# Deformable convolution: patches cut from a turned image in DRAM instead of strips turned tile by tile

## The chip, the cores and the metric

One NeuronCore of a Trainium2 chip runs the whole program. The metric is device time in microseconds (us), as a median of repeated runs. All data is float32.

## The reference

The input `x` is 4 images of 128 channels and 32x32 pixels. Two residual layers follow each other.

1. `x = x + mix(gn(x))`: `gn` normalises groups of 4 channels. `mix` forms the cosine similarity of all 1024 pixels with each other, takes relu and square, and multiplies the result with a 1x1 convolution of the normalised image.
2. `x = x + relu(deform(h))` with `h = gn(x)`: a 3x3 convolution `w1` and a 3x3 convolution `w2` give 72 offset planes (4 groups of channels, 9 taps, y and x). For each pixel, tap and group `h` is read bilinearly at the shifted place (zero outside the image), and a 3x3 convolution `wd` sums the 9 taps.

```
val = gather(y0, x0) * (wy0 * wx0) + gather(y0, x0 + 1) * (wy0 * wx1)
    + gather(y0 + 1, x0) * (wy1 * wx0) + gather(y0 + 1, x0 + 1) * (wy1 * wx1)
out = relu(einsum('ogck,bgckhw->bohw', wd, val))
```

## The kernel before

**Sampling as matrix products.** No gather is used. A tile is 4 rows of the image (128 pixels), so a batch has 8 tiles (`ROWT`). A tile has 8 blocks of 4x4 pixels. With offsets of at most 2 pixels, all that a block reads lies in an 8x8 patch (64 cells) around it, taken from an image whose rows run on into each other and which is wrapped at its ends. For each pixel, tap and group VectorE (DVE) forms the 64 bilinear weights (`tents`, `weights`, lines 1439 to 1474, into `wpix`, in 5 groups of taps). TensorE (PE) turns them from pixel to cell rows (`turn_weights`, line 719) into `psT`, and ScalarE (ACT) copies each group to `wcell` (`evacuate`, line 1005). PE then multiplies the patches with them (`sample`, line 742) in two halves per tile into `psV`, ACT copies these into `val` (line 1018), and `dconv` or, in the last batch, `dconv_tile` applies `wd`.

**How the patches arise before the change.** `wrap_image` on GpSimd (POOL) copies the normalised image `hpad` into `hring` (line 468). For each tile `cut_strips` copies two strips of it, even and odd blocks (line 482). `cut_windows` on PE turns these with 4 transposes into a `psT` bank (line 709). ACT copies the bank into `hwin` (line 999). The even blocks then lie in partitions 0 to 63 and the odd ones in 64 to 127. As `sample` wants each block in both halves, `cross` sends each half to the other with two transfers of 128 KB on the SP queue (line 365). `hwin` has two buffers, for even and odd tiles.

**Order.** All engines follow an order written out by hand. A batch is 72 slots, 9 per tile (`SLOTS`). The text calls the turns of one tile T0, T1, W, T2, T3, T4 (weights 0 to 4, W for the windows), in slots 0, 1, 2, 3, 5, 6 of the tile (`TURN_SLOT`), and S0, S1 the two halves of `sample` for the tile before, in slots 2 and 6. The six turns use the two `psT` banks in turn; each waits until ACT has emptied the bank two turns back (`turns`, line 694).

Between these slots stands the work of later batches: scores and mixing of batch b+2 (`SCORE`, `MIX`, slots 0 to 26; ACT relu, POOL square at line 459), normalising batch b+1 for its second layer (slots 23 to 28), its two convolutions in split precision (`conv_front`: DVE forms row combinations at lines 1263 and 1267 with an ACT copy at line 975 between, PE multiplies at line 540, slots 36 to 41 and 49 to 54), and the offsets: POOL wraps them, the SP queue shifts them by tap with 9 transfers of 8 rows (`shift_offsets`, line 316), PE turns them (line 661, slots 65 and 67). Ahead of batch 0 stands a lead of 72 slots that does the same for batches 0 to 2. Batch 3 has no later batch beside it; there PE has sampling and `dconv_tile` alone.

The SP queue is one ordered list: `shift_offsets(0)`, then for each batch `cross` of tiles 0 to 6, `shift_offsets(b + 1)`, `cross` of tile 7, and the stores.

`sim` (two buffers of 128x1024) holds the squared scores and later, as `off_ring`, the offsets.

Of the kernel before, what the change touches and what calls it, by code (L numbers as in the profile page):

```python
# [37 lines left out]
def mix_deform_kernel(nc, x, W0, b0, w1, b1, w2, b2, wd, out):  # L38
# [17 lines left out]
    HRING = NPIX + 2 * RING  # L56
    V, PAIRS = 4, H // 2
# [5 lines left out]
    TURNS = ["taps 0", "taps 1", "windows 0", "taps 2", "taps 3", "taps 4"]  # L63
    TURN_SLOT = {0: "taps 0", 1: "taps 1", 2: "windows 0", 3: "taps 2", 5: "taps 3", 6: "taps 4"}
# [9 lines left out]
    with ctx:  # L74
# [68 lines left out]
        hring = sb("hring", [P, HRING])  # L143
# [5 lines left out]
        strips = sb("strips", [P, NBLK // 2, 2, CELLS])  # L149
# [79 lines left out]
        def middle_rows(b):  # L229
# [12 lines left out]
            "stat2_done cells_ready w2_ordered off_wrapped off_shifted off_saved hring_done strips_done val_wrapped "  # L242
            "g_off g_offT g_pos g_stat g_h g_hT g_hTs g_place g_shift g_d1 g_f1 g_tent g_zero g_cur g_plane g_turn g_planeT "
            "g_sample g_acc g_conv g_relu g_out g_stored "
            "swap_ready own_ready crossed_even crossed_odd dist_done fold_done tent_done weights_done turned turn_free "
            "sampled val_free dconv_done orelu_done yout_done settled grid_ready out_first out_second").split()}
        out_sems = [s["out_first"], s["out_second"]]
        off_scr = nc.dram_tensor("off_scr", [B, NOFF, NPIX], F32, kind="Internal").ap()

# [16 lines left out]
        LEAD_IMAGE = 37  # L266
# [71 lines left out]
        def _(sp):  # L338
# [21 lines left out]
            def cross(b, t):  # L360

                sp.wait_ge(s["own_ready"], ROWT * b + t + 1)
                for r in range(2):
                    here, there = (slice(CELLS * h, CELLS * (h + 1)) for h in (r, 1 - r))
                    sp.dma_start(hwin[there, t % 2, :, 1, :], hwin[here, t % 2, :, 0, :])\
                        .then_inc(s["crossed_odd" if t % 2 else "crossed_even"], 16)
# [12 lines left out]

            shift_offsets(0)  # L380
            for b in range(B):
                for t in range(ROWT - 1):
                    cross(b, t)
                if b + 1 < B:
                    shift_offsets(b + 1)
                else:
                    store_tile(0)
                cross(b, ROWT - 1)
# [21 lines left out]
        def _(pool):  # L410
# [52 lines left out]
            def wrap_image(b):  # L463

                pool.wait_ge(s["h_done"], b + 1)
                if b > 0:
                    pool.wait_ge(s["strips_done"], 2 * ROWT * b)
                pool.tensor_copy(hring[:, RING:RING + NPIX].rearrange("p (r c) -> p r c", c=WID),
                                 hpad[:, 1:1 + H, 1:1 + WID]).then_inc(s["hring_done"], 1)
                pool.wait_ge(s["hring_done"], 3 * b + 1)  # L470
                pool.tensor_copy(hring[:, 0:RING], hring[:, NPIX:NPIX + RING]).then_inc(s["hring_done"], 1)
                pool.tensor_copy(hring[:, RING + NPIX:HRING], hring[:, RING:2 * RING]).then_inc(s["hring_done"], 1)
                pool.wait_ge(s["hring_done"], 3 * b + 3)

            def cut_strips(b, t):

                if b > 0 or t > 0:
                    pool.wait_ge(s["turned"], (ROWT * b + t - 1) * TGROUPS + TURNS.index("windows 0") + 1 + TURNED0)
                for odd in range(2):
                    at = P * t + BLK * odd  # L480
                    src = hring[:, at:at + SUP * WID].rearrange("p (r m c) -> p m r c", r=SUP, c=SUP)
                    pool.tensor_copy(strips[:, :, odd, :].rearrange("p m (r c) -> p m r c", c=SUP), src)\  # L482
                        .then_inc(s["strips_done"], 1)
# [16 lines left out]
            def batch_steps(b):  # L500
                nxt = b + 1 if b + 1 < B else None
                for t in range(ROWT + 1):
                    for k in range(K):
# [5 lines left out]
                        if t < ROWT - 1 and k == 5:  # L509
                            cut_strips(b, t + 1)  # L510
                        if nxt is not None and t == ROWT - 1 and k == 1:
                            wrap_image(nxt)
                        if nxt is not None and t == ROWT - 1 and k == 5:
                            cut_strips(nxt, 0)
# [6 lines left out]
            for n in range(SLOTS):  # L521
                if n in SCORE:
                    square(0, SCORE.index(n))
                if n == LEAD_IMAGE:
                    wrap_image(0)
                    cut_strips(0, 0)
# [9 lines left out]
        def _(pe):  # L536
# [100 lines left out]
            def conv(b, which, w_p, width, step):  # L637

                for m in (2 * step, 2 * step + 1):
# [63 lines left out]
            def cut_windows(b, t, part):  # L703

                pe.wait_ge(s["strips_done"], 2 * (ROWT * b + t) + 2)
                bank = turns(b, t, f"windows {part}")
                for v in range(4):
                    strip = strips[:, v, :, :].rearrange("p e q -> p (e q)")
                    last = pe.transpose(bank[:, v * C:(v + 1) * C], strip, ident[:, :])  # L709
                last.then_inc(s["turned"], 1)  # L710
# [12 lines left out]
            def sample(b, t, v):  # L723

                n = VGROUPS * t + v
                if v == 0:

                    pe.wait_ge(s["turn_free"], freed(ROWT * b + t, TGROUPS - 1))
                    pe.wait_ge(s["crossed_odd" if t % 2 else "crossed_even"], 32 * (ROWT // 2 * b + t // 2 + 1))
# [107 lines left out]
            def batch_steps(b):  # L837
# [5 lines left out]
                for t in range(ROWT):  # L843
                    for k in range(K):
                        n = K * t + k
                        if k in TURN_SLOT:
                            kind, i = TURN_SLOT[k].split()
                            (turn_weights if kind == "taps" else cut_windows)(b, t, int(i))
# [11 lines left out]
                        if prep is not None:  # L860
                            for what in PREP.get(n, ()):
                                prepare(prep, what)
                        if nxt is not None:
# [37 lines left out]
            for n in range(SLOTS):  # L901
                mix_front(0, n)
                for b, table in ((1, PREP_SECOND), (2, PREP_THIRD)):
                    for what in table.get(n, ()):
                        prepare(b, what)
                conv_front(0, n, LEAD, None)
# [11 lines left out]
        def _(act):  # L918
# [65 lines left out]
            def evacuate(b, t, what):  # L984

                idx = TURNS.index(what)
                kind, i = what.split()
                i = int(i)
# [9 lines left out]
                if kind == "windows":  # L998
                    act.activation(hwin[:, t % 2, :, 0, :], bank.rearrange("q (m c) -> q m c", c=C), ACT.Copy)\
                        .then_inc(s["turn_free"], 1)  # L1000
                    act.wait_ge(s["turn_free"], freed(ROWT * b + t, idx))
                    act.nop().then_inc(s["own_ready"], 1)
                else:
                    taps = TAPS[i]
                    act.activation(wcell[:, t % 2, taps[0]:taps[-1] + 1, :, :].rearrange("q k h p -> q (k h p)"),  # L1005
                                   bank[:, 0:len(taps) * G // 2 * P], ACT.Copy).then_inc(s["turn_free"], 1)
# [48 lines left out]
            def batch_steps(b):  # L1055
                nxt = b + 1 if b + 1 < B else None
                for t in range(ROWT):
                    for k in range(K):
# [10 lines left out]
                        if nxt is not None:  # L1069
                            conv_front(nxt, n, STEADY)  # L1070
                        if b == LAST and t >= 4 and k == 4:
# [24 lines left out]
            for n in range(SLOTS):  # L1096
                mix_front(0, n)
                for b, table in ((1, PREP_SECOND), (2, PREP_THIRD)):
                    for what in table.get(n, ()):
                        prepare(b, what)  # L1100
                conv_front(0, n, LEAD)
# [15 lines left out]
        def _(dve):  # L1117
# [62 lines left out]
            def normalise_x1(b):  # L1180
# [5 lines left out]
                else:  # L1186
                    dve.wait_ge(s["hring_done"], 3 * b)
# [507 lines left out]
```

## Time and profile before

| | us |
|---|---|
| median of 3 runs | 474.54 |
| lowest, highest run | 472.19, 474.91 |
| profiled execution, its own time | 476.88 |
| span of its trace, first to last instruction | 475.2 |

The profiled execution lies 2.34 us above the median. Its mean granted TensorE clock is 0.962 of full speed. Every row of the trace comes from this one execution; times in rows count from the start of the span. In the rows an engine's busy time is the union of its instructions, and the idle time before a group is put down to what ended it.

### The profile page before, as it was taken

To read this page: it belongs to the slowest core of one execution; us is meant where nothing else is said; L and a number is where in the kernel's file an instruction comes from. 1 tells how busy PE (TensorE), PEld (TensorE's weight loads), DVE (VectorE), ACT (ScalarE), POOL (GpSimd) and SP (SyncE) were. 2 spreads that over 40 slices of the span, in tenths; PEclk is the share of its full clock that TensorE was granted. 3 is DMA by queue.
4 is the path that set the end of the run, shared out by engine and by line. 5 is a ranking of instruction groups with operands and counts; after the bars stand their busy time and mean duration, and the time that the engine had idled before them with its cause. 6 is when DMAs were issued, how large, how long until landed. Compare 5 with 4: busy or idle time off the path is not lost.

```text
span 475.2 us, 9943 instructions
## 1 busy us (share of the span) xinstructions
PE 423.5 (89%) x3983; PEld 306.1 (64%) x3983; DVE 344.4 (72%) x586; ACT 230.5 (49%) x416; POOL 131.3 (28%) x171
## 2 busy tenths in 40 slices
PE   7897999989997889899999789799789898979996
PEld 6654657656664665778666566677556566757876
DVE  4994776949999987398755988096977927599701
ACT  3442245155564554443666554433754643167762
POOL 5562472003883111102774110201301120022200
PEclk9997999999999899999999899889988997999999
DMA  7100000021111011311111111401211122022221
GB/s 254 63 0 0 0 3 0 1 50 23 23 23 24 14 20 25 62 25 44 23 22 23 24 24 23 96 12 51 51 23 24 24 41 56 33 57 47 46 63 31
DMA packets 22763, 17.25 MB, mean 36 GB/s; under 512 B 2044, under 2 KB 21244, under 8 KB 22716
## 3 DMA queue, kind: packets, MB, share of 16 engines
q1 hardware_dynamic: 22652, 16.46, 14.9%
q8 instruction: 33, 0.54, 0.4%
q10 hardware_dynamic: 64, 0.13, 0.2%
q14 instruction: 14, 0.11, 0.1%
HBM read 3.74 MB, written 3.28 MB: 15 GB/s over the span
## 4 chain that ended last, share of the span: by engine, by line
PE 54%; DVE 29%; ACT 5%; issue 5%; SPq 3%; POOL 1%; DMA 1%; ACTq 1%; DVEq 0%; POOLq 0%
PE psB L768 10%; PE psB L540 9%; PE psT L719 7%; DVE wpix L1474 6%; PE psV L742 6%; PE psA L540 5%; PE psA L631 4%; DVE combo L1263 3%; DVE tent L1455 2%; PE psT L709 2%; SPq L316 2%; DVE tent L1449 2%; ACT wcell L1005 2%; PE psB L793 2%; DVE combo_p L1267 2%
## 5 line engine op out<-in xcount | busy, mean ns | idle before, releaser
L1005 ACT ACTIVATE wcell<-psT 128x512 f32<-128x512 f32 (+1 forms) x160 | 83.9, 552 | 72.1 <-PE psT L719 70.6
L1474 DVE TENSOR_TENSOR wpix<-tent 128x512 f32<-128x512 f32 (+1 forms) x160 | 104.1, 701 | 14.2 <-PE psT L719 13.1
L719 PE MATMUL psT<-ident,wpix 128*128 128x128 f32 x576 | 88.4, 285 | 13.1 <-ACT wcell L1005 12.0
L719 PEld LDWEIGHTS psT<-ident,wpix 128*128 128x128 f32 x576 | 68.2, 147 | 36.8 <-issue 29.0
L482 POOL COPY strips<-hring 128x256 f32<-128x256 f32 x64 | 40.8, 664 | 145.3 <-PE psT L709 145.2
L459 POOL TENSOR_TENSOR sim<-rel 128x512 f32<-128x512 f32 x48 | 61.8, 1309 | 66.4 <-ACT rel L955 66.4
L1018 ACT ACTIVATE val<-psV 128x576 f32<-128x576 f32 x64 | 44.0, 688 | 22.1 <-PE psV L742 19.7
L768 PE MATMUL psB<-val,wd_sb 128*128 128x256 f32 x216 | 51.6, 394 | 0.0
L742 PE MATMUL psV<-wcell,hwin 64*32 64x144 f32 x2048 | 47.6, 296 | 0.9 <-ACT val L1018 0.9
L631 PE MATMUL psA<-sim,scratch 128*128 128x512 f32 x96 | 47.5, 619 | 0.7 <-POOL sim L459 0.6
L768 PEld LDWEIGHTS psB<-val,wd_sb 128*128 128x128 f32 x216 | 41.0, 195 | 8.6 <-issue 3.1
L540 PE MATMUL psA<-combo_p,w_p 128*128 128x512 f32 (+1 forms) x144 | 43.4, 443 | 1.1 <-DVE combo_p L1267 1.1
L540 PE MATMUL psB<-g_p 128*128 128x512 f32 x144 | 41.6, 424 | 0.0
L955 ACT ACTIVATE rel<-psB 128x512 f32<-128x512 f32 x48 | 28.5, 598 | 24.1 <-PE psB L540 20.2
L540 PE MATMUL psB<-combo_p,w_p 128*128 128x512 f32 (+1 forms) x144 | 38.1, 411 | 0.0
L742 PEld LDWEIGHTS psV<-wcell,hwin 64*32 64x32 f32 x2048 | 28.0, 108 | 13.8 <-issue 10.9
L975 ACT ACTIVATE combo_p<-combo 128x544 fp32r<-128x544 f32 x32 | 20.8, 657 | 28.5 <-DVE combo L1263 28.5
L540 PEld LDWEIGHTS psA<-combo_p,w_p 128*128 128x128 f32 (+1 forms) x144 | 24.9, 183 | 12.0 <-issue 2.6
L709 PE MATMUL psT<-ident,strips 128*128 128x128 f32 x128 | 20.4, 283 | 12.7 <-ACT wcell L1005 12.7
L540 PEld LDWEIGHTS psB<-g_p 128*128 128x128 f32 x144 | 26.0, 191 | 8.2 <-issue 3.4
L1267 DVE TENSOR_TENSOR combo_p<-combo,combo_p 128x544 fp32r<-128x544 f32 x32 | 25.3, 792 | 6.2 <-ACT combo_p L975 5.4
L540 PEld LDWEIGHTS psB<-combo_p,w_p 128*128 128x128 f32 (+1 forms) x144 | 23.3, 166 | 9.9 <-DVE combo_p L1267 0.2
(196 smaller groups left out, 521.9 us busy)
## 6 DMA issues: line engine op xcount, KB each, us to landing
hwin<-hwin SPq DMA_DIRECT2D x64, 128.0 KB, 2.4
x_all<-x SPq DMA_DIRECT2D x1, 1536.0 KB, 10.9
out<-yout SPq DMA_DIRECT2D x12, 128.0 KB, 1.8
off_scr<-sim SPq DMA_DIRECT2D x4, 288.0 KB
combo<-sim SPq DMA_DIRECT2D x32, 32.0 KB
val<-w SPq DMA_DIRECT2D x1, 576.0 KB, 6.2
wd_sb<-wd SPq DMA_DIRECT2D x1, 576.0 KB
x_all<-x SPq DMA_DIRECT2D x1, 512.0 KB, 3.3
```

The costliest lines, as they stand in the source:

```text
L459: pool.tensor_tensor(own.sim[:, i % 2, j * HALF:(j + 1) * HALF], own.rel[:, j, :], own.rel[:, j, :], ALU.mult)\
L482: pool.tensor_copy(strips[:, :, odd, :].rearrange("p m (r c) -> p m r c", c=SUP), src)\
L540: last = pe.matmul(dst, left[l], right[r], start=start and i == 0, stop=stop and i == 2)
L631: last = pe.matmul(own.sums[:, j, :], own.gx[:, i, :], own.sim[:, i % 2, j * HALF:(j + 1) * HALF], start=i == 0, stop=i == QT - 1)
L709: last = pe.transpose(bank[:, v * C:(v + 1) * C], strip, ident[:, :])
L719: last = pe.transpose(bank[:, at:at + P], wpix[:, t % 2, k, 2 * h:2 * h + 2, :].rearrange("p g q -> p (g q)"), ident[:, :])
L742: last = pe.matmul(bank[g * CG:(g + 1) * CG, e, :, m, :], hwin[rows, t % 2, u // 2, (u + r) % 2, g * CG:(g + 1) * CG], w[:, :, :, BLK * u: ...
L768: last = pe.matmul(bank, wd_sb[:, k * C:(k + 1) * C], val[:, k, at:at + 2 * P], start=k == 0, stop=k == K - 1)
L1005: act.activation(wcell[:, t % 2, taps[0]:taps[-1] + 1, :, :].rearrange("q k h p -> q (k h p)"), bank[:, 0:len(taps) * G // 2 * P], ACT.Cop ...
L1018: act.activation(dst, src, ACT.Copy).then_inc(s["val_free"], 1)
L1267: dve.tensor_tensor(combo_p[:, 1, v], combo[:, v % 2], combo_p[:, 0, v].bitcast(F32), ALU.subtract)\
L1474: dve.tensor_tensor(w, ty, tx, ALU.mult).then_inc(s["weights_done"], 1)
```

## The change

The turns of the strips go from the tiles to once per batch. POOL copies `hpad` flat (`copy_flat`, slot 34 of the lead, 28 of a batch). PE turns the image of a batch with 8 transposes into both banks of `psB` (`turn_image`, slot 38 or 33). ACT copies the two banks into buffer 0 of `sim` (`copy_image`, slot 39 or 34). The SP queue stores it as 1024 rows of 512 bytes, with wrapped ends, in DRAM (`store_image`), lays that out as 8 strips of 36 rows of 8 pixels in a second DRAM tensor (`lay_image`, two transfers DRAM to DRAM), and for each tile brings the patches with four transfers of 128 KB (`windows`). These wait until the tile two before has been sampled. W, `cut_strips`, the ring and `cross` are gone, so a tile has 5 turns. New waits: the third row product of the first convolution waits for the copied image (it reuses `psB`), and the offsets wait until the image is stored (they reuse `sim`).

```diff
-    TURN_SLOT = {0: "taps 0", 1: "taps 1", 2: "windows 0", 3: "taps 2", 5: "taps 3", 6: "taps 4"}
+    TURN_SLOT = {0: "taps 0", 1: "taps 1", 3: "taps 2", 5: "taps 3", 6: "taps 4"}
...
-        LEAD_IMAGE = 37
+        LEAD_IMAGE, STEADY_IMAGE, IMAGE_TILE = 38, 33, 5
+        LEAD_FLAT, STEADY_FLAT = 34, 28
...
+            def store_image(b):
+                sp.wait_ge(s["image_copied"], 2 * (b + 1))
+                ring = h_ring[b]
+                sp.dma_start(ring[RING:RING + NPIX, :].rearrange("(i q) c -> q i c", q=P), h_px).then_inc(s["image_stored"], 16)
+                sp.dma_start(ring[0:RING, :], h_px[P - RING:P, QT - 1, :]).then_inc(s["image_stored"], 16)
+                sp.dma_start(ring[RING + NPIX:HRING + BLK, :], h_px[0:RING + BLK, 0, :]).then_inc(s["image_stored"], 16)
+            def lay_image(b):
+                sp.wait_ge(s["image_stored"], 3 * 16 * (b + 1))
+                for odd in range(2):
+                    sp.dma_start(h_scr[b].rearrange("(m e) q c -> e m (q c)", e=2)[odd].rearrange("m (r n) -> m r n", n=SUP * C),
+                                 h_ring[b][BLK * odd:BLK * odd + IMAGE_ROWS * WID, :]
+                                 .rearrange("(r m c) n -> m r (c n)", m=NBLK // 2, c=SUP)).then_inc(s["image_laid"], 16)
+            def windows(b, t):
+                n = ROWT * b + t
+                if t == 0:
+                    sp.wait_ge(s["image_laid"], 2 * 16 * (b + 1))
+                if n >= 2:
+                    sp.wait_ge(s["sampled"], VGROUPS * (n - 1) + SAMPLED0)
+                for odd in range(2):
+                    src = h_scr[b][:, BLK * SUP * t:BLK * SUP * t + CELLS, :].rearrange("(m e) q c -> e q m c", e=2)[odd]
+                    for r in range(2):
+                        dst = hwin[CELLS * r:CELLS * (r + 1), t % 2, :, (odd + r) % 2, :]
+                        sp.dma_start(dst, src).then_inc(s["windows_odd" if t % 2 else "windows_even"], 16)
...
+            store_image(0)
+            lay_image(0)
+            for t in range(2):
+                windows(0, t)
             shift_offsets(0)
             for b in range(B):
+                for t in range(2, ROWT):
+                    if t == IMAGE_TILE and b + 1 < B:
+                        store_image(b + 1)
+                    if t == IMAGE_TILE + 1 and b + 1 < B:
+                        lay_image(b + 1)
+                    if t == ROWT - 1 and b + 1 < B:
+                        shift_offsets(b + 1)
+                    if t == ROWT - 1 and b == LAST:
+                        store_tile(0)
+                    windows(b, t)
...
+                    for t in range(2):
+                        windows(b + 1, t)
                     for m in range(4):
                         store(b, m)
...
+            def copy_flat(b):
+                pool.wait_ge(s["h_done"], b + 1)
+                if b > 0:
+                    pool.wait_ge(s["image_turned"], 2 * b)
+                pool.tensor_copy(h_flat[:, :].rearrange("p (r c) -> p r c", c=WID), hpad[:, 1:1 + H, 1:1 + WID])\
+                    .then_inc(s["flat_done"], 1)
...
+                    if kx == 0 and which == 0 and v == 2:
+                        pe.wait_ge(s["image_copied"], 2 * (b + 1))
...
+            def turn_image(b):
+                pe.wait_ge(s["flat_done"], b + 1)
...
+                for i in range(QT):
+                    last = pe.transpose(psB[:, i // 4, i % 4 * C:(i % 4 + 1) * C], h_flat[:, i * P:(i + 1) * P], ident[:, :])
+                    if i % 4 == 3:
+                        last.then_inc(s["image_turned"], 1)
...
+            def copy_image(b):
...
+                for j in range(2):
+                    act.wait_ge(s["image_turned"], 2 * b + j + 1)
+                    act.activation(h_px[:, 4 * j:4 * j + 4, :].rearrange("p i c -> p (i c)"), psB[:, j, :], ACT.Copy).then_inc(s["image_copied"], 1)
...
+                if which:
+                    dve.wait_ge(s["image_stored"], 3 * 16 * (b + 1))
```

## Rows read from the trace of the kernel before

**Rows 1.** The page: busy us, share of the span, instructions.
```profile
PE 423.5 (89%) x3983; PEld 306.1 (64%) x3983; DVE 344.4 (72%) x586; ACT 230.5 (49%) x416; POOL 131.3 (28%) x171
```

**Rows 2.** The page: the chain that ended last, by engine and by line.
```profile
PE 54%; DVE 29%; ACT 5%; issue 5%; SPq 3%; POOL 1%; DMA 1%; ACTq 1%; DVEq 0%; POOLq 0%
PE psB L768 10%; PE psB L540 9%; PE psT L719 7%; DVE wpix L1474 6%; PE psV L742 6%; PE psA L540 5%; PE psA L631 4%; DVE combo L1263 3%; DVE tent L1455 2%; PE psT L709 2%; SPq L316 2%; DVE tent L1449 2%; ACT wcell L1005 2%; PE psB L793 2%; DVE combo_p L1267 2%
```

**Rows 3.** Groups by line: busy us, mean ns; idle us before, releaser.
```profile
L709 PE MATMUL psT<-ident,strips 128*128 128x128 f32 x128 | 20.4, 283 | 12.7 <-ACT wcell L1005 12.7
```

**Rows 4.** PE in order of time, batch 3, one tile: start, us, instructions.
```profile
421.05 1.06 PE L719 MATMUL psT<-ident,wpix 128*128 128x128 f32 x8 [0.28 <-DVE wpix L1474]
422.52 0.63 PE L709 MATMUL psT<-ident,strips 128*128 128x128 f32 x4 [0.40 <-ACT wcell L1005]
423.07 0.72 PE L742 MATMUL psV<-wcell,hwin 64*32 64x144 f32 x32
...
425.60 0.72 PE L742 MATMUL psV<-wcell,hwin 64*32 64x144 f32 x32
426.25 0.98 PE L719 MATMUL psT<-ident,wpix 128*128 128x128 f32 x7
```

**Rows 5.** PE in order of time, batch 3, a tile with dconv.
```profile
439.06 0.60 PE L709 MATMUL psT<-ident,strips 128*128 128x128 f32 x4
439.59 0.72 PE L742 MATMUL psV<-wcell,hwin 64*32 64x144 f32 x32
```

**Rows 6.** PE in order of time, batch 1, a tile with scores.
```profile
224.09 0.60 PE L709 MATMUL psT<-ident,strips 128*128 128x128 f32 x4
224.53 0.60 PE L719 MATMUL psT<-ident,wpix 128*128 128x128 f32 x4
```

**Rows 7.** PE in order of time, first convolution in batch 0.
```profile
162.02 0.63 PE L709 MATMUL psT<-ident,strips 128*128 128x128 f32 x4 [0.59 <-ACT wcell L1005]
...
163.23 1.73 PE L540 MATMUL psA<-combo_p,w_p 128*128 128x512 f32 x6
```

**Rows 8.** ACT in order of time, the same stretch.
```profile
160.17 0.66 ACT L975 ACTIVATE combo_p<-combo 128x544 fp32r<-128x544 f32 x1 [3.02 <-DVE combo L1263]
...
161.30 1.07 ACT L1005 ACTIVATE wcell<-psT 128x512 f32<-128x512 f32 x2
```

**Rows 9.** PE in order of time, second convolution in batch 0.
```profile
173.65 0.63 PE L709 MATMUL psT<-ident,strips 128*128 128x128 f32 x4 [1.51 <-ACT wcell L1005]
...
178.90 0.41 PE L719 MATMUL psT<-ident,wpix 128*128 128x128 f32 x2
```

**Rows 10.** ACT in order of time, the same stretch.
```profile
178.17 1.56 ACT L1005 ACTIVATE wcell<-psT 128x512 f32<-128x512 f32 x3
```

**Rows 11.** DVE `tent` in batch 2: ns min/median/max, first and last start.
```profile
L1455 DVE SCALAR_TENSOR_TENSOR tent<-tent x3: 758/832/833, 329.2 to 339.6; 128x576 f32<-128x576 f32 x3
```

**Rows 12.** The lead, PE and POOL in order of time.
```profile
67.84 2.43 PE L540 MATMUL psA<-combo_p,w_p 128*128 128x512 f32 x9 [0.65 <-DVE combo_p L1267]
...
67.47 2.61 POOL L459 TENSOR_TENSOR wpix<-wcell 128x512 f32<-128x512 f32 x2 [0.35 <-ACT wcell L955]
70.02 1.53 POOL L468 COPY hring<-hpad 128x1024 f32<-128x1024 f32 x1
```

**Rows 13.** The lead, ACT and the SP queue in order of time.
```profile
72.16 0.66 ACT L975 ACTIVATE combo_p<-combo 128x544 fp32r<-128x544 f32 x1 [2.29 <-DVE combo L1263]
...
94.89 3.41 SPq L316 DMA_DIRECT2D combo<-sim  x5
```

**Rows 14.** DMA: 40 slices of the span; issues; packets between 94 and 103 us.
```profile
DMA  7100000021111011311111111401211122022221
GB/s 254 63 0 0 0 3 0 1 50 23 23 23 24 14 20 25 62 25 44 23 22 23 24 24 23 96 12 51 51 23 24 24 41 56 33 57 47 46 63 31
...
hwin<-hwin SPq DMA_DIRECT2D x64, 128.0 KB, 2.4
...
DMA packets 228, 0.59 MB, mean 66 GB/s; under 512 B 84, under 2 KB 84, under 8 KB 228
```

More of the change, by code:

```diff
@@ L461, in square @@
                         .then_inc(s["sim_done"], 1)
-            def wrap_image(b):
+            def copy_flat(b):
                 pool.wait_ge(s["h_done"], b + 1)
                 if b > 0:
[L467 to L483, printed above, removed]
+                    pool.wait_ge(s["image_turned"], 2 * b)
+                pool.tensor_copy(h_flat[:, :].rearrange("p (r c) -> p r c", c=WID), hpad[:, 1:1 + H, 1:1 + WID])\
+                    .then_inc(s["flat_done"], 1)
             def wrap_offsets(b):
@@ L508, in batch_steps @@
                             wrap_offsets(nxt)
[L509 to L514, printed above, removed]
+                        if nxt is not None and n == STEADY_FLAT:
+                            copy_flat(nxt)
                         if t in (1, ROWT) and k == 8:
@@ L701, in turns @@
                 return psT[:, (TGROUPS * t + idx) % 2, :]
[L703 to L710, printed above, removed]
+            def turn_image(b):
+                pe.wait_ge(s["flat_done"], b + 1)
+                if b > 0:
+                    pe.wait_ge(s["orelu_done"], 4 * (b - 1) + ORELU0)
+                if b + 1 < B:
+                    pe.wait_ge(s["rel_done"], 2 * QT * (b + 2 if b else 1))
+                for i in range(QT):
+                    last = pe.transpose(psB[:, i // 4, i % 4 * C:(i % 4 + 1) * C], h_flat[:, i * P:(i + 1) * P], ident[:, :])
+                    if i % 4 == 3:
+                        last.then_inc(s["image_turned"], 1)
             def turn_weights(b, t, i):
@@ L862, in batch_steps @@
                                 prepare(prep, what)
+                        if nxt is not None and n == STEADY_IMAGE:
+                            turn_image(nxt)
                         if nxt is not None:
@@ L905, in _ @@
                         prepare(b, what)
+                if n == LEAD_IMAGE:
+                    turn_image(0)
                 conv_front(0, n, LEAD, None)
@@ L986, in evacuate @@
                 idx = TURNS.index(what)
-                kind, i = what.split()
-                i = int(i)
+                i = int(what.split()[1])
                 if idx == 0:
@@ L997, in evacuate @@
                 bank = psT[:, (TGROUPS * t + idx) % 2, :]
[L998 to L1006, printed above, removed]
+                taps = TAPS[i]
+                act.activation(wcell[:, t % 2, taps[0]:taps[-1] + 1, :, :].rearrange("q k h p -> q (k h p)"),
+                               bank[:, 0:len(taps) * G // 2 * P], ACT.Copy).then_inc(s["turn_free"], 1)
+            def copy_image(b):
+                if b > 0:
+                    act.wait_ge(s["off_saved"], 16 * b)
+                    act.wait_ge(s["off_shifted"], SHIFTS * b)
+                if b + 1 < B:
+                    act.wait_ge(s["mix_done"], QT * (b + 2 if b else 1))
+                for j in range(2):
+                    act.wait_ge(s["image_turned"], 2 * b + j + 1)
+                    act.activation(h_px[:, 4 * j:4 * j + 4, :].rearrange("p i c -> p (i c)"), psB[:, j, :], ACT.Copy)                        .then_inc(s["image_copied"], 1)
             def take_samples(b, t, v):
@@ L1070, in batch_steps @@
                             conv_front(nxt, n, STEADY)
+                        if nxt is not None and n == STEADY_IMAGE + 1:
+                            copy_image(nxt)
                         if b == LAST and t >= 4 and k == 4:
@@ L1100, in _ @@
                         prepare(b, what)
+                if n == LEAD_IMAGE + 1:
+                    copy_image(0)
                 conv_front(0, n, LEAD)
```

40 lines of the change are left out of this document (15 added, 25 removed).

## The prediction

> **What bounds the kernel now.** I read the page first. TensorE is busy for 89% of the span and no other engine is over 72% [rows 1]. That is a mean over stages, so I took the chain of waits next: 54% of it lies on PE and 29% on DVE [rows 2], so time taken from PE comes back where PE ends last, and is lost where DVE or ACT does. The turning of the windows, W, holds 2% of the chain by itself. The list of groups gives its whole size: 20.4 us of PE time in 128 transposes, and 12.7 us in which PE stood idle before them until ACT had emptied a bank of `psT` [rows 3]. Last I went through PE and ACT in order of time, stage by stage, to see which wait ends last there.
>
> **What W is worth, stage by stage.** In the new order S0 follows T1 directly, and T2 and T3 wait for banks that were filled one turn earlier than before, so no wait for a bank gets longer.
>
> - Batch 3, tiles without `dconv` (four, the last one half): T0 and T1 end at 422.11, PE idles 0.40, and W takes 0.55 until S0 starts at 423.07 [rows 4]. Both go, as S0 needs nothing of T0's bank; T0 is copied while S0 runs. I take 0.9 of the 0.95, so 3.6. The period of 5.20 [rows 4] becomes 4.3.
> - Batch 3, tiles with `dconv_tile` (four): PE never idles, and W takes 0.53 from its start to S0's [rows 5]. 4 x 0.53 = 2.1.
> - Batch 1, slots 0 to 26: PE is full with scores and mixing. W takes 0.44 [rows 6]; three tiles, 1.3.
> - Batch 0, same slots: DVE is on the chain, not PE. What comes is relief from POOL's copying of strips. Where POOL runs no squares, `tent` line 1455 takes 0.758 us alone and 0.833 beside such copies [rows 11]; two DVE operations per tile touch them, 0.15 per tile. Three tiles, 0.5. The first three tiles of batch 2 are bound by DVE too: 0.5. Nothing and three times as much are the ends.
> - First convolution (batches 0, 1 and 2): PE idles 0.59 for a bank and W takes 0.56, with the next row product only at 163.23 [rows 7]. ACT is late, as it waited until 160.17 for DVE's last row combination [rows 8]. S0 then waits only for the copy of the samples before, which ACT makes ahead of that bank. The new `copy_image` puts two copies, 1.07 as in [rows 8], between them; T2, one row product later, covers it. 1.1 each, 3.3; and 0.7 in batch 2, where W of tile 3 also holds up the ACT copy from which the first row product comes.
> - Second convolution (three times): PE idles 1.51 before W at 173.65 [rows 9], which looks like the best gain, but is not: T4 at 178.90 starts just after ACT's copy of T2 ends (178.17 + 0.58) [rows 9, 10], and ACT copies in order behind DVE's row combinations. What PE wins at 173.65 it loses at 178.90. I take 0.25 each, 0.7.
> - Tile 7 of batch 0: W and its wait, of which the offsets' turns give half back, 0.45. In batches 1 and 2 PE waits there for the shifted offsets; nothing.
>
> Sum: 3.6 + 2.1 + 1.3 + 0.5 + 0.5 + 3.3 + 0.7 + 0.7 + 0.45 = 13.15 saved. POOL's strips, ACT's copies of W and the crossings leave engines that bind nowhere; they are costed at nothing beyond the relief above.
>
> **What comes in.** (a) `turn_image`, 8 transposes, 1.06 as the first line of [rows 4]. In batches 0 to 2 it stands before the first convolution, where PE waits for row combinations anyway; these are made after `hpad`, as is the flat copy. That cover is a tie, 0 to 0.3 each; I take 0. (b) In the lead the cover is too short. The flat copy comes before the square that ran from 67.47, and lasts 1.53 [rows 12], so to 69.0 at most; turning ends at 69.9, and the convolution that began at 67.84 [rows 12] starts 1.5 to 2 late. (c) `copy_image(0)` stands behind the last of ACT's four copies of row combinations, which ends at 72.82 [rows 13]: image copied at 73.9. The third row product, before at 73.00 and now about 1.6 later, just meets that.
>
> (d) The path through DRAM in the lead. The SP queue must store the image, lay it, and issue eight window transfers before `shift_offsets(0)`, which began at 94.89 [rows 13]. An issue takes 3.41/5 = 0.68; a 128 KB transfer lands 2.4 after its issue [rows 14]. The store has four times the data: about 4.6 with its three issues, so 78.5. Laying moves 8 x 36 x 4 KB = 1.18 MB. In the first slice all 16 DMA engines, busy for 7 tenths, moved 254 GB/s [rows 14], so 363 GB/s busy throughout: 3.3 us on 16 engines. But not every transfer uses 16. Between 94 and 103 us nine shifts of 8 rows and one store of 72 rows moved 144 large pieces and closed with 84 small packets [rows 14]: 9 x 8 and 12. So a transfer runs on as many engines as divide its rows. The laying's outermost extent is 4 strips, with 36 pieces in each; whether the pieces spread, no row tells. With 4 engines laying takes 13.0, with 16 it takes 3.3. I take 13.0, as in all these the closing packets divide the outer extent. With 2 us to land, the image lies at 93.5, the windows are issued by 98.9, and the shift starts 4.0 late. Of that PE waited 0.6 less, so the lead loses 3.4, which includes (b). Ends: 1.6 (16 engines) and 9 (DRAM to DRAM at two thirds of that rate).
>
> The Trainium skill's page "DMA: Bandwidth & Descriptors", section "Why a DMA increments its semaphore by 16 and not by 1", speaks against the change here: it lets a transfer use the largest number up to 16 that divides the slowest extent of both sides, which for 4 strips gives 4. By that rule the sum stays as it is; by the other reading it would be 1.8 better.
>
> (e) In later batches the same laying starts when the window transfers of tile 5 are issued, 20 us ahead of its use, and is over before the next shift. Nothing. (f) Window transfers: four issues and a landing are 3 x 0.68 + 2.4 = 4.4 from the trigger; one after another they would take 9.6. The trigger is the end of S1 of tile t-2; S0 of tile t comes two periods after the S0 that stands 3.25 before this end [rows 4]. At a period of 4.3 that leaves 2 x 4.3 - 3.25 = 5.35, in tiles with scores over 15. I take 4.4, since the two crossings, issued 0.6 apart, both land in 2.4: transfers overlap. So nothing waits. (g) Stores of batch b now queue behind the windows of the next batch, which wait for S1 of tile 7; output rows have two buffers and `dconv` lasts longer than the delay. Nothing.
>
> Net: -13.15 + 3.4 = -9.75. The profiled execution, 476.88 in all, would become 467.1. It lies 2.34 above the median of 474.54, so against the runs I forecast **464.8 us**.
>
> **Rivals.** *More comes back (454).* W's 2% of the chain (9.5 us) and all 12.7 us of idle time before it [rows 2, 3] are saved and the laying runs on 16 engines: -22.2 + 1.6 = -20.6. For it: waits often vanish together. Against: rows 9 and 10. Chance 0.13.
>
> *The time is handed to DVE and ACT (472).* In the three batches with convolutions each gain is met by a later wait, as in [rows 9, 10], and only batch 3 keeps its 5.7: -5.7 + 3.4 = -2.3. For it: DVE's 29% of the chain. Against: rows 6 and 7, where PE has work queued and nobody late. Chance 0.13.
>
> *The windows come late (slower, 486).* Place: the first product of S0. If four transfers take L, the period cannot be below (L + 3.25)/2. In batch 3 and the first tiles of batch 2 ten tiles have periods of 5.2 (six) or 6.1 (four). Without batch 3's share the rest nets -7.45 + 3.4, about -4. The loss 6 x (P - 5.2) + 4 x (P - 6.1) eats this at P = 6.0, so L = 8.7; that is the point. At L = 11 P is 7.1, the loss 15.6, the time 486. For it: one after another gives 9.6. Against: they overlap today. Chance 0.08.
>
> **Numbers.** The forecast has 0.66; its own range is 459 to 470 (saving 10.5 to 16, lead 1.6 to 9, not both ends at once). To leave out no more than 2 in 10 I reach to 456 and 471, into the first two rivals. About 1%, 4.7 us, is what a measurement tells from no change, so faster means under 469.8: 0.62 of the forecast, 0.13 and a little of the second, 0.78. Same: 0.13. Slower: the third and a lead that loses more than 16, 0.09.
>
> **What would show it.** Right: tiles of batch 3 at periods near 4.3 and 5.6; in the second convolution T4 still starting on ACT's copy; `shift_offsets(0)` about 4 us later, with the laying's packets over 13 us. Wrong: PE idle before S0 with a DMA as releaser; the laying done in 4 us; PE waiting for POOL's flat copy in batches 0 to 2; a lower granted clock where PE now idles more.

## The result, and the profile after

The changed kernel takes **459.79 us** (median of 4 runs, 459.05 to 463.93) beside 474.73 for the kernel before, measured beside it: a ratio of 0.969, 95% interval 0.965 to 0.974. Five later runs (E0 below) gave 461.14 and 0.970 (0.968 to 0.972). The forecast was 464.8, the range 456 to 471. The direction and the main mechanism held; 4 to 5 us more came back than the sum had, and some terms of the sum missed in opposite directions.

The profiled execution took 459.05 us, span 457.0, mean granted clock 0.970. From its page: busy time, the chain by engine and by line [rows 1, 2], and from the groups by line the one that holds the window transfers' only wait.

```profile
PE 405.2 (89%) x3887; PEld 291.9 (64%) x3887; DVE 339.5 (74%) x586; ACT 215.6 (47%) x392; POOL 90.0 (20%) x99
...
PE 46%; DVE 32%; DMA 6%; SPq 5%; issue 4%; ACT 4%; POOL 1%; DVEq 0%; ACTq 0%; POOLq 0%
...
L762 PE MATMUL psV<-wcell,hwin 64*32 64x144 f32 x2048 | 47.2, 294 | 3.9 <-ACT val L1045 3.5 <-DMA hwin<-h_scr 0.4
```

PE's share of the chain fell from 54% to 46%; DVE, DMA and the SP queue took it over. PE waited for windows 0.4 us in all in this execution, so step (f) and the third rival are settled.

PE in batch 3: a tile without `dconv` [rows 4], then one with it [rows 5].

```profile
411.11 1.09 PE L739 MATMUL psT<-ident,wpix 128*128 128x128 f32 x8
412.13 0.72 PE L762 MATMUL psV<-wcell,hwin 64*32 64x144 f32 x32
...
414.26 0.41 PE L739 MATMUL psT<-ident,wpix 128*128 128x128 f32 x2 [0.39 <-ACT wcell L1021]
...
415.25 1.09 PE L739 MATMUL psT<-ident,wpix 128*128 128x128 f32 x8
...
425.15 0.38 PE L739 MATMUL psT<-ident,wpix 128*128 128x128 f32 x2
425.46 0.72 PE L762 MATMUL psV<-wcell,hwin 64*32 64x144 f32 x32
...
430.82 0.38 PE L739 MATMUL psT<-ident,wpix 128*128 128x128 f32 x2
```

S0 follows T1 with no wait. The period is 415.25 - 411.11 = 4.14, against a forecast of 4.3; with `dconv` it is 430.82 - 425.15 = 5.67, against 5.57.

First convolution of batch 1, made during batch 0: PE [rows 7] and ACT [rows 8].

```profile
158.09 1.71 PE L555 MATMUL psA<-combo_p,w_p 128*128 128x512 f32 x6
160.50 0.72 PE L762 MATMUL psV<-wcell,hwin 64*32 64x144 f32 x32 [0.69 <-ACT val L1045]
161.15 1.25 PE L555 MATMUL psA<-combo_p,w_p 128*128 128x512 f32 x4
...
159.12 0.66 ACT L998 ACTIVATE combo_p<-combo 128x544 fp32r<-128x544 f32 x1 [3.02 <-DVE combo L1294]
159.68 0.67 ACT L1045 ACTIVATE val<-psV 128x576 f32<-128x576 f32 x1
160.24 1.07 ACT L1033 ACTIVATE sim<-psB 128x512 f32<-128x512 f32 x2
```

As forecast, S0 waits only for the copy of the samples before, and the image's two copies (1.07) stand behind that. Ahead of this stretch lies a cost that the sum had at nothing. DVE's first two row combinations after `hpad`, before and then changed, with POOL's flat copy:

```profile
153.26 1.36 DVE L1263 TENSOR_TENSOR combo<-hpad 128x544 f32<-128x544 f32 x2
```

```profile
151.54 2.20 DVE L1294 TENSOR_TENSOR combo<-hpad 128x544 f32<-128x544 f32 x2
151.57 1.59 POOL L502 COPY h_flat<-hpad 128x1024 f32<-128x1024 f32 x1 [8.86 <-DVE hpad L1219]
```

Both start from `hpad`. The second combination takes 1.56 beside the flat copy, 0.72 without it (in the lead, where POOL's squares run beside it, 1.56 in both kernels). T0 of tile 4, which waits for ACT behind these combinations, comes 4.37 after `hpad` in place of 3.53, in batches 0 and 1 of every trace of the changed kernel and of its variants.

Second convolution of the same batch, PE and ACT [rows 9, 10]:

```profile
176.42 0.41 PE L739 MATMUL psT<-ident,wpix 128*128 128x128 f32 x2 [0.88 <-ACT wcell L1021]
...
175.70 1.55 ACT L1021 ACTIVATE wcell<-psT 128x512 f32<-128x512 f32 x3
```

T4 still starts just after ACT's first copy (175.70 + 0.58). The lead [rows 12, 13]: PE, then ACT, then the SP queue; last, 10 us of the laying by windows (span, busy of PE, PEld, DVE, ACT and POOL, granted clock, DMA share, GB/s).

```profile
66.17 1.09 PE L728 MATMUL psB<-ident,h_flat 128*128 128x128 f32 x8 [1.46 <-POOL h_flat L502]
67.01 1.72 PE L555 MATMUL psA<-combo_p,w_p 128*128 128x512 f32 x6
...
100.73 0.34 PE L678 MATMUL psA<-ident,combo 72*128 72x72 f32 x2 [1.06 <-DMA combo<-sim]
...
70.25 1.07 ACT L1033 ACTIVATE sim<-psB 128x512 f32<-128x512 f32 x2
...
75.32 1.26 SPq L376 DMA_DIRECT2D h_scr<-h_ring  x2
89.69 5.44 SPq L391 DMA_DIRECT2D hwin<-h_scr  x8
95.18 3.49 SPq L320 DMA_DIRECT2D combo<-sim  x5
...
78.00:88.00 10.00, 10.00 (x61) 7.59 (x60) 7.16 (x12) 5.44 (x9) 0.00 (x0) 1.00 0.26 104
```

The work ahead of the change already ran 2.48 us earlier in this execution than in that of before (`hpad` at 60.68 against 63.16; the work up to there is the same), so stages are compared by their own lengths. From PE's first weight turn of one batch to that of the next (the lead from `hpad`, batch 3 to the end of the span), with the second profiled run of the changed kernel (E0 below), and with two kernels that come later (E12 and E10):

```
          before   changed          forecast   measured       E12      E10     E10-E12
lead       45.78    47.74  46.68     +3.4     +1.95 +0.90     45.79    47.40    +1.61
batch 0   111.18   108.19 109.75     -2.3     -2.99 -1.43    112.68   108.16    -4.52
batch 1   107.37   102.28 102.33     -2.65    -5.09 -5.04    106.77   101.37    -5.40
batch 2    89.28    84.69  84.64     -2.55    -4.59 -4.64     85.49    79.98    -5.51
batch 3    58.39    53.44  53.70     -5.7     -4.95 -4.69     58.71    52.70    -6.01
```

Two sizes were off: the lead lost less, and batches 1 and 2 gained nearly twice as much as forecast.

### The profile page after: what moved, and what is told of

The parts are those of the page before. It is cut to its first block, busy times and chain, and to the rows that moved or that the text cites. A ratio compares the mean times of both kernels' runs of the same rounds, so it can differ in the third digit from the quotient of the medians.

```text
span 457.0 us, 9689 instructions
## 1 busy us (share of the span) xinstructions
PE 405.2 (89%) x3887; PEld 291.9 (64%) x3887; DVE 339.5 (74%) x586; ACT 215.6 (47%) x392; POOL 90.0 (20%) x99
## 4 chain that ended last, share of the span: by engine, by line
PE 46%; DVE 32%; DMA 6%; SPq 5%; issue 4%; ACT 4%; POOL 1%; DVEq 0%; ACTq 0%; POOLq 0%
PE psB L788 10%; PE psB L555 9%; PE psT L739 7%; DVE wpix L1507 7%; PE psV L762 5%; DVE combo L1294 4%; PE psA L646 4%; DMA h_scr<-h_ring 3%; SPq L320 3%; DVE combo_p L1298 2%; DVE tent L1488 2%; PE psA L555 2%; DVE tent L1482 2%; PE psB L813 2%; PE psA L813 2%
## 5 line engine op out<-in xcount | busy, mean ns | idle before, releaser
L1507 DVE TENSOR_TENSOR wpix<-tent 128x512 f32<-128x512 f32 (+1 forms) x160 | 99.7, 675 | 14.4 <-PE psT L739 13.3
L646 PE MATMUL psA<-sim,scratch 128*128 128x512 f32 x96 | 45.6, 597 | 0.6 <-POOL sim L493 0.6
L555 PE MATMUL psA<-combo_p,w_p 128*128 128x512 f32 (+1 forms) x144 | 40.7, 423 | 0.0
L555 PEld LDWEIGHTS psA<-combo_p,w_p 128*128 128x128 f32 (+1 forms) x144 | 23.5, 172 | 9.5 <-issue 1.3
L646 PEld LDWEIGHTS psA<-sim,scratch 128*128 128x128 f32 x96 | 17.6, 190 | 15.6 <-issue 12.1
L1488 DVE SCALAR_TENSOR_TENSOR tent<-tent 128x576 f32<-128x576 f32 x32 | 26.4, 825 | 1.1
```

The lines of the kernel that those rows point to most:

```text
L555: last = pe.matmul(dst, left[l], right[r], start=start and i == 0, stop=stop and i == 2)
L646: last = pe.matmul(own.sums[:, j, :], own.gx[:, i, :], own.sim[:, i % 2, j * HALF:(j + 1) * HALF], start=i == 0, stop=i == QT - 1)
L1488: dve.scalar_tensor_tensor(out=tent[:, :, :], in0=tent[:, :, :], scalar=-1.0, in1=tent[:, :, :], op0=ALU.mult, op1=ALU.min).then_inc(s["fo ...
L1507: dve.tensor_tensor(w, ty, tx, ALU.mult).then_inc(s["weights_done"], 1)
```

## The experiments

**Theory**: TensorE's W and its wait for a bank are the saving, POOL's relief is about 1, and the lead loses through the order of the SP queue. **Rivals**: POOL and the crossings carried it; or something that the sum left out (the clock).

**E4, W's PE time alone.** In `turn_weights`, after the wait for the bank:

```diff
+                if i == 2:
+                    for v in range(4):
+                        pe.transpose(bank[:, v * C:(v + 1) * C], ident[:, :], ident[:, :])
```

> The changed kernel with four idle transposes of the identity ahead of the third turn of every tile, in the same bank, so that TensorE alone gets W's work back; no bank, copy, strip or crossing comes back. Theory (PE's time is what was saved where PE ends last): 8 tiles of batch 3 at 0.5, 3 tiles of batch 1 at 0.44, about 0.5 in each of the four first-convolution stretches, 0 to 1 elsewhere: +7, 467. Rival (the saving came from ACT or POOL): 0 to +1, 460 to 461.

462.11 (460.75 to 466.09), ratio 0.975 (0.966 to 0.984): 1 to 2.3 over the changed kernel, where 7 was expected. The interval holds the changed kernel's 0.970, so the times alone show no difference; the rows do. The rival (460 to 461) did not fit either. PE in a tile of batch 3 of this kernel:

```profile
414.74 0.72 PE L765 MATMUL psV<-wcell,hwin 64*32 64x144 f32 x32
415.39 0.66 PE L738 MATMUL psT<-ident 128*128 128x128 f32 x4
415.88 1.04 PE L742 MATMUL psT<-ident,wpix 128*128 128x128 f32 x8
```

Each tile pays 415.88 - 415.39 = 0.49, less 0.05 of a wait that shrank: the first two tiles of batches 0, 1 and 2 and most of batch 3 take some 0.4 longer each (2.4 in batch 3). Between batches it is returned: the last tile of batch 1 is 1.35 shorter than in E0, that of batch 2 3.1. This kernel's mean granted clock is 0.983, E0's 0.966. Work added to PE was paid for in part by a better clock; that made the clock the rival to test.

**E5, W's bank and ACT copy too.**

```diff
+    TURNS = ["taps 0", "taps 1", "windows 0", "taps 2", "taps 3", "taps 4"]
...
+                for v in range(4):
+                    last = pe.transpose(bank[:, v * C:(v + 1) * C], ident[:, :], ident[:, :])
...
+                    act.activation(spared[:, :], bank, ACT.Copy).then_inc(s["turn_free"], 1)
```

> The changed kernel with W's whole turn back between the second and the third: a bank of psT, four transposes (of the identity) and an ACT copy of 128x512 into a tile that nobody reads. POOL's strips and the crossings stay out. Theory (W and its bank are the saving, POOL's relief is 1): +12, 472, with batch 3's tiles at 5.1 and 6.1 again. Rival (most of it came from POOL and the crossings): at most +7, 467.

474.18 (471.53 to 477.23, 10 runs), ratio 0.998 (0.994 to 1.002): no longer to be told from the kernel before. PE in batch 3 has rows 4's pattern again, the wait before W included, at a period of 426.62 - 421.50 = 5.12:

```profile
421.50 1.09 PE L747 MATMUL psT<-ident,wpix 128*128 128x128 f32 x8
422.91 0.66 PE L737 MATMUL psT<-ident 128*128 128x128 f32 x4 [0.31 <-ACT wcell L1034]
423.49 0.72 PE L770 MATMUL psV<-wcell,hwin 64*32 64x144 f32 x32
...
426.62 1.09 PE L747 MATMUL psT<-ident,wpix 128*128 128x128 f32 x8
```

The turn with its bank is worth about the whole net change (13 to 14); neither the windows' new path nor the crossings are needed to explain it. That the totals agree so closely is in part luck: in batch 2 the turn costs nothing (84.38 against 84.69 in the changed kernel), where the granted clock is 0.98 in place of 0.92.

**E6, POOL's strips alone** (`cut_strips` back, reading `h_flat` and writing a tile that nobody reads).

```diff
+                for odd in range(2):
+                    src = h_flat[:, at:at + SUP * WID].rearrange("p (r m c) -> p m r c", r=SUP, c=SUP)
+                    pool.tensor_copy(strips[:, :, odd, :].rearrange("p m (r c) -> p m r c", c=SUP), src)
```

> The changed kernel with POOL's two strip copies per tile back, at the old place and on the old trigger, into a tile that nobody reads; nothing else comes back. Theory (they touch only DVE operations beside them, 0.15 a tile where DVE is on the chain): +0.5 to +1.5, 461. Rival (POOL's strips were what held DVE): +5 or more, 465 and up.

463.88 (463.53 to 465.30), ratio 0.978 (0.972 to 0.984): 2.7 to 4.1 over the changed kernel, between the two. The groups by line (busy, mean ns, idle before) of E6 and then of the changed kernel:

```profile
L1523 DVE TENSOR_TENSOR wpix<-tent 128x512 f32<-128x512 f32 (+1 forms) x160 | 104.1, 701 | 13.3 <-PE psT L755 12.2
```

```profile
L1507 DVE TENSOR_TENSOR wpix<-tent 128x512 f32<-128x512 f32 (+1 forms) x160 | 99.7, 675 | 14.4 <-PE psT L739 13.3
```

The strips make `wpix` on DVE 26 ns slower each, 4.4 in all. Batch 3 is no longer for it than in E0, and the first six tiles of batch 0 take 0.6 more, none of it in its first three tiles. The rest lies between batches and in batch 2, where low stretches of the clock differ from E0's (0.960 on the mean); so whether POOL's relief is worth 1 or 3 stays open.

**E7, windows loaded twice, one after the other.**

```diff
+                for twice in range(2 if n >= 2 else 1):
+                    sp.wait_ge(done, max(128 * (ROWT // 2 * b + t // 2) - 64 * (1 - twice), 0))
```

> The changed kernel with the four window transfers of every tile from the third on issued twice, the second time after the first has landed, so that a load takes about 8.8 in place of 4.4. Theory (a load that fits into two periods less 3.25 costs nothing, a longer one sets the period at (L + 3.25)/2 = 6.0): batch 3 goes from 4.2 to 6.0 in three or four tiles and from 5.65 to 6.0 in four, +7 to +9, 467 to 469, with PE waiting for the transfers ahead of S0. Rival (windows have slack to spare everywhere): 0, 460.

516.63, ratio 1.091 (1.083 to 1.098). Both missed. The SP queue at the end of batch 2, and in batch 3, which begins at 441.28:

```profile
388.80 1.31 SPq L376 DMA_DIRECT2D h_scr<-h_ring  x2
390.21 17.15 SPq L394 DMA_DIRECT2D hwin<-h_scr  x8
407.41 6.11 SPq L320 DMA_DIRECT2D combo<-sim  x9
...
449.93 40.58 SPq L394 DMA_DIRECT2D hwin<-h_scr  x40
```

The wait for the first load sits on the queue, so loads of two tiles no longer overlap: 40.58 for five tiles, 8.1 each. Batch 3 keeps its pace for three tiles and then runs at 34.8/4 = 8.7 a tile on the mean, not 6.0, partly at half speed (its mean granted clock is 0.86). Eight issues behind the laying took 17.15 and held the shift of the offsets back: laying and windows meet when the queue has no slack. In batch 2 of the changed kernel the windows of tile 6 go out 5.9 after the laying, the shift 14.0 and the windows of tile 7 and of the next batch 20.6, and PE's wait for windows is the 0.4 above. So (e) and (f) hold there, but the formula of the third rival is not tested.

**E1, laying with 36 rows outermost; E2, shift ahead of the windows.**

```diff
-.rearrange("m (r n) -> m r n", n=SUP * C)   ... "(r m c) n -> m r (c n)"
+.rearrange("m (r n) -> r m n", n=SUP * C)   ... "(r m c) n -> r m (c n)"
```

```diff
+            shift_offsets(0)
             for t in range(2):
                 windows(0, t)
-            shift_offsets(0)
```

> The changed kernel with the laying's axes in another order: 36 rows outermost and 4 strips inside, in place of 4 and 36; same bytes, same pieces. Theory (a transfer runs on the largest number up to 16 that divides its outer extent: 12 in place of 4): the laying lands after some 6 in place of 14.4, windows are issued by 88, and the shift starts when the wrapped offsets are there, 93.45, which is 1.7 earlier than now: 458. Rival (the engines are bound by the strips or by the bytes): laying and time as they are, 459.8.

> The changed kernel with the first batch's shift of the offsets ahead of the eight window transfers on the SP queue; the laying stays as it is. Theory (the lead loses its 1.7 only through the queue's order): the shift starts at 93.45 in place of 95.18, windows land by 106, well before the first sample: 458. Rival (the lead's loss lies in the later start of the convolution): 459.8.

E1 460.84, ratio 0.968 (0.964 to 0.971); E2 461.39, 0.970 (0.967 to 0.973): no difference from the changed kernel. The mechanism is there all the same. E1, the SP queue and windows in the laying:

```profile
76.87 1.59 SPq L376 DMA_DIRECT2D h_scr<-h_ring  x2
84.07 5.29 SPq L391 DMA_DIRECT2D hwin<-h_scr  x8
94.97 3.44 SPq L320 DMA_DIRECT2D combo<-sim  x5
...
78.00:83.00 5.00, 5.00 (x32) 4.04 (x31) 2.32 (x4) 2.86 (x6) 0.00 (x0) 1.00 0.68 229
```

From issue to windows the laying takes 7.20 in place of 14.37, at a DMA share of 0.68 in place of 0.26, by these shares some 11 and 4 of 16 engines. The shift comes 32.73 after `hpad` in E1 and in E2, as the wrapped offsets allow, against 34.50 in the changed kernel's first profile. But the late shift costs less than noise of the clock: batch 0 began 0.97 earlier than in the changed kernel's first profile in E2, 0.69 later in E1, where the clock was low just behind the shift, and in E0, without any edit, 1.06 earlier.

**E3, the image turned after T0 of tile 4** (`STEADY_IMAGE` 36 in place of 33).

> The changed kernel with the image of the next batch turned three steps later, behind the first weight turn of tile 4 and ahead of the convolution. Theory (PE's wait for POOL's flat copy, 0.8 in each of batches 0 to 2 at T0 of tile 4, is given back by tile 5, because DVE's row combinations set the pace): T0 of tile 4 comes 0.8 earlier and the time stays, 459 to 460. Rival (it is on the chain): 457.5.

463.08, ratio 0.976 (0.972 to 0.979), slower by 2 to 3. T0 did not come earlier; the theory's premise was wrong. PE, and the windows row of the same place one batch later:

```profile
156.88 1.08 PE L739 MATMUL psT<-ident,wpix 128*128 128x128 f32 x4 [4.62 <-ACT wcell L1021]
...
262.00:269.00 7.00, 5.68 (x23) 5.02 (x23) 6.86 (x12) 3.68 (x7) 0.00 (x0) 0.51 0.17 49
```

T0 waits for ACT, which stands behind DVE's row combinations (4.37 after `hpad` here too), so the turn itself was covered, as (a) had it; the flat copy that slows these combinations was not. Moved away, the turn stands ahead of the convolution, and PE has one wait of 4.62 in place of 2.77, and one batch later, with a wait of 3.97, the clock is at half speed (1.2 GHz) for 7 us.

**E9, all three.**

> The laying on 12 engines, the shift ahead of the windows and the later turn together. Theory: no more than the shift's 1.7, since the first two end at the same wait for the wrapped offsets: 458. Rival (they add): 455 to 456.

464.03, ratio 0.975 (0.971 to 0.978). Worse than E1 and E2, as E3 is in it.

**E0, E10, E11: the clock.** E10 puts idle transposes into the waits of PE that its expectation lists; E11 adds E2's edit. Shown is one of the places.

```diff
+        FILL_IMAGE, FILL_TAPS, FILL_VAR, FILL_SHIFT = (0, 18, 14, 0), 18, 24, 12
...
+            def fill(bank, count):
+                for i in range(count):
+                    pe.transpose(bank, ident[:, :], ident[:, :])
...
+                if FILL_IMAGE[b]:
+                    pe.wait_ge(s["sd_done"], b + 1)
+                    fill(psB[:, 0, 0:P], FILL_IMAGE[b])
                 pe.wait_ge(s["flat_done"], b + 1)
```

> The changed kernel once more, beside the next two on the same chip, to have their yardstick: 459 to 462.

> The changed kernel with idle transposes of the identity in five waits of TensorE that last 1.9 to 4.3 (18 and 14 ahead of the image's turn for batches 1 and 2, 18 ahead of the last weight turn of tile 6 in batch 0, 24 ahead of the second group mean in batch 2, 12 ahead of the offsets' turn in batches 1 and 2), each count shorter than its wait. Theory (in the changed kernel TensorE idles longer and the half clock that follows these waits costs 1.5 to 3 each where PE has work): the low stretches near 153, 259, 300, 334 and 381 go, 3 to 7 less, 453 to 457. Rival (the clock falls elsewhere as often, or PE does not end last there): 459 to 461; with the fillers in the way, up to 463.

> The same fillers with the first batch's shift of the offsets ahead of the window transfers. Theory (the shift 1.8 earlier is worth its size once the clock does not fall behind it): 1.5 less than with the fillers alone, 452 to 456. Rival (the lead's gain is eaten by DVE's pace in batch 0): as with the fillers alone.

E0 461.14 (ratio 0.970, 0.968 to 0.972), E10 **454.07** (0.955, 0.953 to 0.957), E11 **453.73** (0.954, 0.952 to 0.956). The granted clock in 40 slices, and two stretches by windows, of E0 and then of E10 (the same work, 1 to 2 us apart):

```profile
PEclk9998999999999899899999899989979997999999
...
186.00:189.00 3.00, 0.37 (x4) 0.14 (x2) 0.78 (x1) 2.19 (x4) 0.00 (x1) 1.00 0.36 70
189.00:193.00 4.00, 3.94 (x40) 2.87 (x41) 1.23 (x1) 2.31 (x4) 0.00 (x0) 0.57 0.37 53
```

```profile
PEclk9896999999999999999999999999999999999999
...
188.00:191.00 3.00, 2.78 (x26) 2.54 (x24) 1.05 (x4) 1.75 (x3) 0.36 (x2) 1.00 0.31 68
191.00:195.00 4.00, 3.50 (x46) 2.84 (x47) 1.23 (x1) 2.64 (x5) 0.00 (x0) 1.00 0.38 53
```

In E0 PE does 0.37 of work in 3 us, and the clock then falls to half (1.2 GHz); with fillers it stays at 2.4 GHz. All six low stretches behind these waits are gone, and 7 us come back: the theory, at its upper end. Tile by tile, E0 against E10, the two stretches at tile 4 of batches 0 and 1 cost nothing (13.9 in both); the other four cost 1.6, 1.0, 1.9 and 2.7. Counted from `hpad`, batch 0 begins 0.6 earlier in E11's trace than in E10's, and the end comes 0.6 earlier; the medians differ by 0.3, too little to tell. The 1.5 was too much.

**E12, the kernel before with fillers in its own waits.**

> The kernel before the change with fillers in the same waits of its own (18 and 14 transposes of the identity ahead of the first weight turn of tile 4 in batches 0 and 1, 18 in tile 6 of batch 0, 8 ahead of the second group mean in batch 2, 12 ahead of the offsets' turn in batches 1 and 2), to compare the two kernels with the clock held in both. Theory (of the 14.9 that the change gave, the part over the sum's is the clock, which fell oftener before): the two are 10 to 12 apart, 464 to 466 beside 454. Rival (the change's own work is worth all of it): 15 apart, 469.

471.67 (468.74 to 474.09, 12 runs), ratio 0.995 (0.992 to 0.998). Both numbers missed: with fillers in both, the kernels are 471.67 - 454.07 = 17.6 apart, more than the 14.9 without (they ran on different chips; each against the kernel before on its own chip, 18.1). But the clock was not held in this kernel, so the test does not decide how much of the change is the clock. PE in batch 0's first convolution of E12, and the clock around it:

```profile
158.87 0.63 PE L709 MATMUL psT<-ident,strips 128*128 128x128 f32 x4 [2.10 <-ACT wcell L1024]
159.43 0.72 PE L747 MATMUL psV<-wcell,hwin 64*32 64x144 f32 x32
...
156.00:160.00 4.00, 1.90 (x40) 1.11 (x38) 4.00 (x8) 2.66 (x5) 0.44 (x1) 1.00 0.00 0
160.00:164.00 4.00, 4.00 (x24) 3.21 (x13) 3.75 (x7) 1.03 (x3) 1.53 (x2) 0.57 0.35 70
```

Here W itself is a wait, 2.10 long, and the clock falls behind it, in all three batches with a convolution (low again at 270 and 355). T0 of tile 4 to T0 of tile 5 takes 16.6 in E12 and 13.9 in E10. Without fillers the clock falls somewhere in both kernels, one wait earlier or later; with them only the changed kernel has no such wait left. The change removed waits that drew the clock down, and by the medians the waits that it left hid some 2.7 of the 17.6. By the stages above, E10's four batches are 21.4 shorter than E12's and its lead 1.6 longer, in one execution of each. What W is worth with the clock held in both kernels no run shows.

## Why the prediction was right, and where its sizes were not

- **W where PE ends last**: right. Batch 3: four tiles without `dconv` gained 3.3 to 3.5 (forecast 3.6), those with it 0.43 each, three of them 1.3, and the last tile 0.1 (2.1 for four): 4.7 to 4.95 of 5.7. Batch 1's first three tiles: 1.6 to T0 of tile 3 (1.3). E4 gave 0.43 a tile for PE's time alone, E5 the whole.
- **Batch 0's first tiles as DVE's**: wrong reading. They gained 1.1, not 0.5, and not through POOL's relief: with the strips back (E6) tiles 0 and 1 take what they take in the changed kernel (11.29 and 12.94), with W's PE time back (E4) 0.42 and 0.43 more. PE was on the chain there. The `tent` that the prediction took to run alone (329.24 to 330.00) also had a strip copy beside it, from 329.62.
- **First convolution and (a)**: the W part was right, and a cost was missed. From T0 of tile 4 to T0 of tile 5 batches 0 and 1 gained 1.2 (forecast 1.1; from 15.1 to 13.9). But T0 of tile 4 itself came 0.84 later after `hpad`, the 0.84 that DVE's row combination lost beside the flat copy, so from `hpad` to T0 of tile 5 only 0.36 is left (18.63 to 18.27, 18.60 to 18.25). (a) asked whether the copy ends in time, not what it does to DVE, and took 0. Whether a later flat copy would bring this back no run tests. In batch 2 tile 4 gained 3.1: before, the clock was low there from 357.6 to 361.0, behind W's wait, as it is in E12. **Second convolution**: 0.4 each (0.25), with T4 on ACT's copy as forecast.
- **Tile 7 of batches 1 and 2 at nothing** (tile 6 was not in the sum): wrong, and the step that was furthest off. From T0 of tile 6 to the next batch batch 1 gained 2.7 and batch 2 1.1; with fillers in both kernels, 1.6 and 1.2. PE's wait for the shifted offsets is as long as before (1.9 at the end of batch 1), but it moved as a whole, and W's 0.5 in tiles 6 and 7 was saved on either side of it. The other 1.1 in batch 1 lies where the clock was low from 306.4 to 313.2 before, and in E0 from 302.1 to 305.5 only.
- **(d) the lead at 3.4**: mis-sized, 0.9 to 1.95. The laying took 13.6 to 14.4 from its issues, 13.0 + 2 in the sum; the rule of the outer extent, worked out from rows 14, held (0.26 of 16 engines with 4 strips outermost, 0.68 with 36 rows). By the rule on the Trainium skill's page "DMA: Bandwidth & Descriptors", section "Why a DMA increments its semaphore by 16 and not by 1", 4 strips give 4 engines and E1's 36 rows give 12. The traces' shares, some 4 and 11 engines, agree as nearly as a mean over a stretch with the start in it can. But the wrapped offsets came 1.0 later themselves (32.73 after `hpad`, 31.73 before), which fits the later convolution of (b), and so the queue was late by only 0.9 to 1.8 against them, not by 4.0 against the old time.
- **(c), (e), (f), (g)**: no cost seen.
- **Rivals**: the third is refuted by 0.4 us of waiting for windows, the second by batches 1 and 2, which gained about as much as batch 3. Of the first (454) part came true: the lead's loss is near its 1.6, though on 4 engines and not 16, and more came back between batches. In the changed kernel as it is, its 22.2 did not show (15.8 to 17.6 in the four batches); between E12 and E10 the batches differ by 21.4, some of which is the clock in E12.
- The sum had one list of PE's time at one speed. What a wait costs behind it, in work at 1.2 GHz, had no term. That the total came within 5 us is helped by luck: W's time in tiles 6 and 7 and in batch 0 was left out or put too low, and the flat copy's 0.84 in batches 0 and 1 was left out on the other side.

## What to carry to other kernels

An instruction group that PE waits for costs its own time, its wait, and sometimes the half clock behind the wait; look at the granted clock of the stretch after each long wait of PE (1.9 to 4.6 us here) before summing. A copy that only has to end in time can still cost what it takes from the engine beside it, so compare the neighbour's rows as well. Short idle work in such waits brought 1.5% here, more than any reordering, and it had to be put into every such wait, for in E12 the clock fell behind those left open. A queue's late transfer is to be measured against what the new order makes the others wait for, not against the old time.

## What the runs showed of the hardware that was not expected

- The same code drew a low clock at different places: behind PE's wait of 2.69 us in batch 0 (tile 6) the clock stayed full in the changed kernel's first profile and fell in E0 (0.57 between 189 and 193). E0's tile 6 takes 1.6 longer for it, as much as some edits here.
- A transfer from DRAM to DRAM went at 104 GB/s with 4 rows outermost and 229 GB/s with 36, bytes and pieces the same.
- POOL copies of 128x256 beside DVE made DVE's 128x512 products slower by 4% on the mean (701 against 675 ns), though they overlap only part of them. A POOL copy of 128x1024 cost more: DVE's 128x544 row combination that started beside it took 1.56 us in place of 0.72, in batches 0 to 2 of every trace of the changed kernel.
